# Building two of every five wide one-hots with a comparison of two tensors in place of a per-partition scalar

## The reference

```
xs, xd = x[src], x[dst]
F_s = householder(reflection(xs, xd));  F_d = householder(reflection(xd, xs))
L_sd  = -einsum('eki,ekj->eij', F_s, F_d)
coef  = deg_inv_sqrt[src] * deg_inv_sqrt[dst]
msg_s = coef * einsum('eij,ej->ei', L_sd, xd)
msg_d = coef * einsum('eji,ej->ei', L_sd, xs)
out   = x - zeros.at[src].add(msg_s) - zeros.at[dst].add(msg_d)
```

## Time and profile before

| | |
|---|---|
| median of 3 runs | 23112.76 us (23050.33 to 23122.42) |
| profiled execution | 23039.02 us, span 23037.1 us |
| busy: PE, DVE, ACT, POOL | 79%, 60%, 27%, 72% of the span |
| gathers of the sheaf layer on POOL | 7817.0 to 14248.2 us |
| DVE's one-hots of the sheaf layer (L1370) | 850, from 8157.9 to 14665.6 us |

### The profile page before, as it was taken

The page is one execution under the profiler, slowest core; times in us unless marked ns, Lnnn a source line. Parts: engine busy times, 40 slices in busy tenths (PEclk is TensorE's granted clock), DMA queues, the critical chain, the costliest instruction groups (busy, mean ns, idle before and its releaser), DMA issues. The chain is left out here.

```text
span 23037.1 us, 291747 instructions
## 1 busy us (share of the span) xinstructions
PE 18150.1 (79%) x98910; PEld 13788.4 (60%) x98910; DVE 13778.7 (60%) x24271; ACT 6244.1 (27%) x8041; POOL 16691.9 (72%) x14269
## 2 busy tenths in 40 slices
PE   0688882699997178888878888389999988999997
PEld 0344442344443167777777777389999986555556
DVE  2788883455554155555555555367777772777772
ACT  0000000000000066777766777311111111111111
POOL 5777774777776588888888887487777751777775
PEclk9888885799998588888888888689999998999998
DMA  2122220111111112111111111122222221888884
GB/s 98 45 61 61 61 62 23 38 42 47 42 43 40 17 30 39 29 29 29 29 31 37 29 29 26 32 52 44 42 41 46 42 32 61 251 252 249 251 252 123
DMA packets 1853618, 1604.27 MB, mean 70 GB/s; under 512 B 671719, under 2 KB 1624198, under 8 KB 1835094
## 3 DMA queue, kind: packets, MB, share of 16 engines
q0 software_dynamic: 781216, 459.51, 13.0%
q10 hardware_dynamic: 821300, 579.22, 8.1%
q1 hardware_dynamic: 249730, 548.09, 7.1%
HBM read 906.08 MB, written 679.64 MB: 69 GB/s over the span
## 5 line engine op out<-in xcount | busy, mean ns | idle before, releaser
L802 POOL DMA_INDIRECT gathered<-gat_table,src_index x4810 | 4829.6, 1004 | 1496.1 <-issue 1471.1
L1444 POOL DMA_INDIRECT acc<-column_sums,sum_rows x2625 | 4815.0, 1834 | 1288.6 <-issue 779.6
L1385 PE MATMUL node_sums<-placed_row,lane_values 128*128 128x392 f32 x22200 | 4480.8, 353 | 7.3 <-DVE placed_row L1343 3.8
L1684 POOL DMA_INDIRECT gathered<-sheaf_table,src_index x3125 | 3554.9, 1138 | 963.3 <-issue 957.4
L1385 PEld LDWEIGHTS node_sums<-placed_row,lane_values 128*128 128x128 f32 x22200 | 3977.7, 190 | 190.2 <-issue 157.9
L2479 POOL DMA_INDIRECT gathered<-message_table,src_index x2381 | 2363.0, 992 | 727.4 <-issue 725.1
L1009 PE MATMUL lanes_ps<-S,table_parts 128*128 128x512 bf16 x9828 | 2266.9, 393 | 334.3 <-DVE S L874 334.3
L1009 PE MATMUL lanes_ps<-code_onehot,table_parts 128*128 128x512 bf16 x9828 | 2217.4, 387 | 156.1 <-DVE code_onehot L874 156.1
L1343 DVE TENSOR_SCALAR placed_row<-iota_rows_f,src_row 128x1568 fp32r<-128x1568 f16 x1500 | 1570.5, 1055 | 848.9 <-PE node_sums L1385 843.7
L1358 ACT ACTIVATE row_distance<-iota_rows_f,src_row 128x1568 bf16<-128x1568 f16 x1275 | 2035.5, 1596 | 25.7 <-issue 10.0
L1009 PEld LDWEIGHTS lanes_ps<-S,table_parts 128*128 128x128 bf16 x9828 | 983.9, 101 | 1554.1 <-DVE S L874 320.3
(11 more groups left out here) (493 smaller groups left out, 26778.9 us busy)
## 6 DMA issues: line engine op xcount, KB each, us to landing
message_rows<-gathered ACTq DMA_DIRECT2D x250, 1600.0 KB, 10.6
src_rows<-src_rows SPq DMA_DIRECT2D x150, 640.0 KB
src_rows<-src_rows SPq DMA_DIRECT2D x100, 960.0 KB
code_rows<-src_code_rows SPq DMA_DIRECT2D x360, 256.0 KB, 3.2
gat_rows<-scanned ACTq DMA_DIRECT2D x25, 3375.0 KB
gathered<-gat_table,src_index POOLq DMA_INDIRECT x4810
gat_rows<-scanned ACTq DMA_DIRECT2D x25, 2125.0 KB
start_values<-starts SPq DMA_DIRECT2D x50, 1062.5 KB, 5.1
```

The lines of the kernel that those rows point to most:

```text
L802: g.indirect_dma_start(G[b][:, j, :], None, tab, bass.IndirectOffsetOnAxis(ap=IX[b][:, j:j + 1], axis=0)).then_inc(s_g[b], 16)
L1385: last = pe.matmul(o.acc[:, m, 0:Q8 // 4], lane, o.OW[r][:, m * (Q8 // 4):(m + 1) * (Q8 // 4)], start=first(k, 1) and i == 0 and part == 0 ...
L1444: g.indirect_dma_start(self.acc[i], bass.IndirectOffsetOnAxis(ap=o.IXS[b][:, j:j + 1], axis=0), o.SV[b][:, j, :], None, compute_op=ALU.add ...
L1684: g.indirect_dma_start(G[b][:, j, :], None, self.tab17, bass.IndirectOffsetOnAxis(ap=IX[b][:, j:j + 1], axis=0)).then_inc(s_g[b], 16)
```

## The change

One instruction is replaced, in `mixed_dve`. Before, the row of the edge was a scalar operand, one value for each partition. Now it is the second of two tensors: the same column, repeated 1,568 times by an access pattern that doesn't step. What is compared, the types, the output buffer, the wait ahead of it and the semaphore behind it stay.

```diff
-        v.tensor_scalar(o.OW[i % o.ring], o.IO16[:], o.LO[b][:, i:i + 1], None, ALU.is_equal).then_inc(o.s_mv, 1)
+        v.tensor_tensor(o.OW[i % o.ring], o.IO16[:], bcast(o.LO[b][:, i:i + 1], [P, Q8]), ALU.is_equal).then_inc(o.s_mv, 1)
```

## The result

The changed kernel takes 23,397.5 us (median of 4 runs, 23,341.2 to 23,404.0), the kernel before beside it 23,098.0 (4 runs, 23,050.3 to 23,122.4): ratio 1.0127 [1.0103, 1.015]. It is slower by about 300 us; the forecast was 318. The profiled execution took 23,341.15 us with a span of 23,339.3, at a granted clock of 0.869 in the mean, against 0.874 before.

A forecast was written before the change was run, and what follows sets the result against it. POOL's queue was taken to pace the chunks at 265.3 us, the computation close behind at 262.6. POOL's 313 us plus the computation's 5 gave 318 on a 23,113 us median, rounded to 23,430; range 23,240 to 23,610.

The forecast's parts named there:

- The duration: On DVE, each one-hot comparison takes 1.79 us in place of 1.06, 0.73 us more.
- The computation's own 5 us: Per chunk, longer one-hots on DVE's path raise the computation's need from 262.6 to 267.6 us; PE hides the rest.
- POOL's price: Each new one-hot holds up POOL's gathers and scatter-adds 0.40 us more than the old: 13.6 us per chunk, 313 in all.
- The sum: Whole kernel: 313 us from POOL plus 5 from the computation, 318 us more, a median of 23,430 us.
- The chunk and its waits: Chunk starts 279 us apart; DVE's wait for gathers at L1835 grows from 62.5 to some 250 us over 22 chunks.
- 0.08 us more each: On POOL, the mean gather and the mean scatter-add each lengthen by 0.08 us, from 13.6 us over 165 instructions.
- The inference of the Trainium skill: On POOL, two-SBUF-input tensor_tensor wouldn't stall descriptor making, so the change would free POOL; the prediction followed the rows instead.
- The new one-hot holding nobody: Rival: POOL loses 16 us less per chunk, the computation paces, 58 us more, 23,170 us; chance 10%.
- The computation in front: Rival: uncovered longer one-hots delay DVE's queue, up to 287.4 us per chunk, 508 us more, some 23,620; chance 12%.
- the instruction that is no longer: Rival: a 16-bit operand keeps DVE's old pace, POOL's loss falls a little, about 23,050 to 23,110 us; chance 4%.

The follow-up runs named there:

- the two runs with 105 gathers: Changed kernel and kernel before, each with 105 of the 125 gathers per chunk of the sheaf layer: 23,086.0 us with the change, 22,995.3 without.
- the gapped rows: Kernel before, scalar comparison kept, its source `IO16` in 7 rows of 224 with gaps of 2 elements: 23,133.6 us, ratio 1.0023 [1.0011, 1.0034].

## Why the prediction was right, step by step

- **The duration.** Forecast 1.79 us by the pace of `equal_src`; measured 1.79.
- **The computation's own 5 us.** Forecast 1.5 at the opening, 0 in the steps, 2.9 in DVE's stretch, 0.6 behind it, together 267.6; measured in one chunk 1.6, 0, 2.8, 0.4, and 267.4. Over 22 chunks the two runs with 105 gathers, where the computation is in front, put the change at 3.7 us; the gapped rows, with one-hots of 1.85 us, lie 266.9 - 262.6 = 4.3 us above the kernel before.
- **POOL's price.** The step on which the forecast stood. The difference of 0.40 us per one-hot, taken below the 0.47 of the sum, was measured as (278.85 - 265.3) / 34 = 0.40, whatever POOL needs without one-hots. Both prices were lower than worked out: 0.43 for 0.48, and 0.83 for 0.95. So the cut that I made for starts that aren't random had the right size, but it was a judgement, and that it met the difference to the second digit is luck. That starts aren't random the trace shows: of the 297 gathers into which a new one-hot alone began, 134 had been running for 0.4 to 0.5 us. That this is what lowers the price was not worked out. One term of the old form's price was a slip: the 0.18 for a scatter-add is a gather's, divided by 1.24 us; by 1.85 it is 0.12, and the weighted price 0.47. The count by the longest overlap, as above, gives 27.5 us per chunk after and 14.4 before, a difference of 0.39 each.
- **The sum.** From the first scatter-add to the last gather POOL ran 6,379 us against 6,071, 308 us more where 313 stood. The profiled executions differ by 302.
- **The chunk and its waits.** 278.85 us against 278.9; the wait at L1835 is 247 us against some 250.
- **What was off.** I gave gather and scatter-add 0.08 us more each. The gather got 0.055, the scatter-add 0.158; 125 x 0.055 + 40 x 0.158 = 13.2 us, so the sum hid it. The new order of meeting explains the split: the 4.32 us of L1885, which before fell on a gather, now falls on a scatter-add, as the last pair of the timelines shows (5.63 us, from 1.55 alone). In the count over 22 chunks L1885 and L1886 took 3.40 us from one gather of each chunk before, and take 4.08 us from one scatter-add after. Without these the gather has 0.055 + 3.40 / 125 = 0.082 us more, and the scatter-add 0.158 - 4.08 / 40 = 0.056: without L1885 the 0.08 fits the gather and is too much for the scatter-add.
- **The inference of the Trainium skill** ("SBUF — State Buffer", section "Who interferes with whom"). That a tensor_tensor with both inputs in SBUF doesn't stall the making of descriptors was set against the rows. The gathers that end 0.82 us after a one-hot, and the fall from 1.0127 to 1.0023 with a longer one-hot that has one SBUF input, decide for the rows. But the section was less against the term than the prediction says: its rule lets such an instruction contend with a GpSimd instruction that reads SBUF, and each gather reads its row numbers there. No run separates that reading from the making of descriptors. The section's rule on instructions with one SBUF input agrees with the gapped run.
- **The rivals.** The new one-hot holding nobody, priced at 58 us over the kernel before, was nearly built by the gapped rows, which took 60: the size was right and the case was not this change's. The computation in front is excluded by POOL's unbroken "issue" and by DVE's waits for gathers, 247 / 22 = 11 us per chunk; the instruction that is no longer, by 1.79 us.

## What to carry to other kernels

An instruction's price is not only its own engine's time: here 0.73 us more on a half idle DVE was hidden nearly everywhere, and the 0.40 us that it took from POOL, which had no idle time, decided. Where two chains lie within 1%, find out which of them an edit touches before adding anything up, and expect the gain from either alone to end at the other, as the four comparisons moved to ACT did. A form that is slower by itself but holds nobody (1.85 us for 1.05) can be the start of a gain, once the other chain is shortened too.

## What the runs showed of the hardware

- A DVE comparison of one 16-bit source of 128 x 1,568 with a scalar takes 1.05 to 1.07 us and holds gathers when the source is one run of 1,568; with the source in 7 rows with gaps it takes 1.845 us and holds none of them (under 0.01 us in the mean of some 900).
- A comparison of two SBUF tensors, one of them a single repeated column, holds a gather that starts under it until 0.82 us after its end (median of 332), but none of the 297 that had started before it took over 1.02 us.
- The scalar form also holds a gather that has just started: begun 0.43 to 0.45 us into it, it makes the gather 1.59 to 1.61 us long (15 cases in the kernel before), begun 0.48 to 0.52 us into it, it leaves it at 0.94 or 0.95 (11 cases).
- Two comparisons of 0.97 us in a row cost POOL less than one of 1.79 us: the kernel's ratio is 1.0022 [1.0013, 1.0032] in place of 1.0127 [1.0103, 1.015].
